# The experts' loads on SyncE: a program without a loop, its row numbers and words read one step ahead

## The reference, cut to what matters

```python
logits = x @ router_w + router_b                  # 8 experts
top_w, sel = jax.lax.top_k(logits, 2)
top_w = jax.nn.softmax(top_w, axis=-1)
...
gu = x @ Wgu + bgu                                # 128 -> 512
gate, up = jnp.split(gu, 2, axis=-1)
act = (up + 1.0) * quick_gelu(gate)
out = act @ Wd + bd                               # 256 -> 128
return (acc + out * w_e[:, None], None)           # only the two chosen experts have a weight
```

## Time and profile before

| | us |
|---|---|
| median of 3 runs | 1164.15 |
| the runs | 1164.15, 1156.54, 1166.43 |
| the profiled execution: its own time | 1155.15 |
| the profiled execution: span from the first to the last instruction | 1153.3 |
| PE busy over the span | 977.3 (85%) |
| DVE busy over the span | 837.6 (73%) |
| ACT busy over the span | 669.9 (58%) |

### The profile page before, as it was taken

The page is one execution under the profiler, slowest core; times in us unless marked ns, Lnnn a source line. Parts: engine busy times, 40 slices in busy tenths (PEclk is TensorE's granted clock), DMA queues, the critical chain, the costliest instruction groups (busy, mean ns, idle before and its releaser), DMA issues. The chain is left out here.

```text
span 1153.3 us, 41735 instructions
## 1 busy us (share of the span) xinstructions
PE 977.3 (85%) x14086; PEld 825.0 (72%) x14086; DVE 837.6 (73%) x2058; ACT 669.9 (58%) x1348; POOL 551.9 (48%) x588
## 2 busy tenths in 40 slices
PE   4799999899996788878888785179999999999995
PEld 3478877777775346666666664079898989889995
DVE  4687777677775246778787786358888888888885
ACT  1276666575661345666766663066676666666663
POOL 0327464647475712556556565414444444444444
PEclk9899999999999677899999997589999999999998
DMA  8011000001100200111121121556666666666661
GB/s 324 20 39 39 30 31 27 29 26 36 45 3 7 105 18 26 50 59 58 60 65 54 60 66 55 100 201 229 232 229 236 225 218 223 227 232 230 229 220 66
DMA packets 87673, 127.68 MB, mean 111 GB/s; under 512 B 12436, under 2 KB 53555, under 8 KB 87533
## 3 DMA queue, kind: packets, MB, share of 16 engines
q1 hardware_dynamic: 75116, 107.08, 26.8%
q0 software_dynamic: 9120, 17.15, 4.8%
q10 hardware_dynamic: 3298, 1.37, 0.8%
HBM read 31.61 MB, written 20.91 MB: 46 GB/s over the span
## 5 line engine op out<-in xcount | busy, mean ns | idle before, releaser
L1360 POOL DMA_INDIRECT out<-e_y,e_xg x156 | 155.6, 998 | 66.1 <-issue 66.1
L1413 PE MATMUL e_ps<-e_xt,weights 128*128 128x128 f16 x624 | 137.7, 221 | 25.6 <-DMA e_fed<-weights 16.5
L254 POOL TENSOR_SCALAR vm<-v,early 128x512 f32<-128x512 f32 x96 | 148.7, 1566 | 0.0
L820 POOL DMA_INDIRECT rows<-m_rows,m_place x128 | 126.9, 992 | 44.2 <-issue 44.2
L1415 PE MATMUL e_ps<-e_xt,weights 128*128 128x128 f16 x624 | 137.7, 221 | 0.0
L1414 PE MATMUL e_ps<-e_xt,weights 128*128 128x128 f16 x624 | 137.2, 220 | 0.0
L1413 PE MATMUL e_ps<-e_xt,e_fed 128*128 128x128 f16 x624 | 137.1, 220 | 0.0
L1414 PE MATMUL e_ps<-e_xt,e_fed 128*128 128x128 f16 x624 | 137.1, 220 | 0.0
L1415 PE MATMUL e_ps<-e_xt,e_fed 128*128 128x128 f16 x624 | 137.1, 220 | 0.0
L1494 DVE SCALAR_TENSOR_TENSOR e_hid<-e_ps,e_act 128x512 f32<-128x512 f32 x156 | 107.0, 686 | 27.9 <-ACT e_act L1479 16.1
L1500 DVE SCALAR_TENSOR_TENSOR e_hid_hl<-e_hid,e_hid_hl 128x512 f16<-128x512 f32 x156 | 108.1, 693 | 16.9 <-ACT e_hid_hl L1473 16.1
(11 more groups left out here) (262 smaller groups left out, 3098.0 us busy)
## 6 DMA issues: line engine op xcount, KB each, us to landing
e_fed<-weights SPq DMA_DIRECT2D x156, 416.0 KB
e_xg<-rows SPq DMA_DIRECT2D x156, 66.5 KB
resid<-in_x SPq DMA_DIRECT2D x8, 1024.0 KB, 14.2
xb<-in_x SPq DMA_DIRECT2D x32, 256.0 KB, 2.6
m_rows<-resid SPq DMA_DIRECT2D x32, 256.0 KB, 2.7
out<-e_y,e_xg POOLq DMA_INDIRECT x156, 3.3
m_w_f<-in_L_ffn_gate_up_proj SPq DMA_DIRECT2D x1, 2048.0 KB, 8.3
rows<-m_rows,m_place POOLq DMA_INDIRECT x128
```

Source lines behind the costliest of these rows:

```text
L254: ins = g.tensor_scalar(vm[:, u, :, n, :], full, pair_of[:, n:n + 1], None, ALU.mult)
L820: g.indirect_dma_start(rows_dram, bass.IndirectOffsetOnAxis(ap=place[:, slot, j:j + 1], axis=0), rows[:, slot, j, :], None).then_inc(s.row ...
L1360: nc.gpsimd.indirect_dma_start(out_rows, bass.IndirectOffsetOnAxis(ap=who, axis=0), y[:, slot, i, :], None, bounds_check=B * TOK - 1, oob_ ...
L1413: t.matmul(o, hi, x2[0], start=True, stop=False)
```

## The change

SP's loop becomes a program written out over all 80 steps of n. The limits of the `value_load`s are dropped, so nothing is checked behind them. The two row numbers of block n + 1 are read behind the two token DMAs of block n (the first two ahead of everything), and the word of the next 8 steps is read behind the last copy that needs the present one. The DMAs, their sizes, their order and the waits for semaphores are the same, with constant counts.

```diff
-            at = lambda n: slice(n, n + 1) if isinstance(n, int) else bass.ds(n, 1)
-            def load(n, slot, rounds):
-                need(sp, r_out[slot], 32 * rounds)
-                for half in range(2):
-                    row = sp.value_load(ffn["first_i"][0:1, half, at(n)], min_val=0, max_val=G * REGION)
-                    sp.dma_start(xg[:, slot, half], rows_dram[bass.ds(row, UNIT)]).then_inc(x_in[slot], 16)
...
-            def second_weights(k, ring, word, digit):
-                e = (word // 8 ** (digit + 1 - 2 * (digit % 2))) % 8
-                need(sp, s.y_psum, k - TURN + 1)
-                sp.dma_start(fed[:, ring:ring + 1], ffn["weights"][:, bass.ds(e, 1)]).then_inc(fed_in[ring], 16)
...
-            eight(0, 0, SLOTS, SLOTS)
-            with sp.Fori(1, BLOCKS // SLOTS) as m:
-                eight(m, 0, SLOTS, SLOTS)
-            for m in range(BLOCKS // SLOTS, -(-(BLOCKS + LEAD) // SLOTS)):
-                eight(m, 0, min(SLOTS, BLOCKS + LEAD - SLOTS * m), BLOCKS - SLOTS * m)
+            def rows_of(n):
+                return [sp.value_load(ffn["first_i"][0:1, half, n:n + 1]) for half in range(2)]
+            def second_words(turn):
+                return sp.value_load(ffn["word_i"][0:1, 1, turn:turn + 1])
+
+            coming, word = rows_of(0), second_words(0)
+            for n in range(BLOCKS + LEAD):
+                if n < BLOCKS:
+                    slot, here = n % SLOTS, coming
+                    need(sp, r_out[slot], 32 * (n // SLOTS))
+                    for half in range(2):
+                        row = here[half]
+                        sp.dma_start(xg[:, slot, half], rows_dram[bass.ds(row, UNIT)]).then_inc(x_in[slot], 16)
+                    if n + 1 < BLOCKS:
+                        coming = rows_of(n + 1)
+                for u in range(2 if n >= LEAD else 0):
+                    k = 2 * (n - LEAD) + u
+                    turn = (k + 2) // TURN
+                    digit = k - TURN * turn + BEHIND
+                    e = (word // 8 ** (digit + 1 - 2 * (digit % 2))) % 8
+                    need(sp, s.y_psum, k - TURN + 1)
+                    sp.dma_start(fed[:, k % TURN:k % TURN + 1], ffn["weights"][:, bass.ds(e, 1)]).then_inc(fed_in[k % TURN], 16)
+                    if (k + 3) // TURN > turn:
+                        word = second_words(turn + 1)
```

More of the change, by code:

```diff
@@ L1306, in _ @@
         def _(sp):
-            at = lambda n: slice(n, n + 1) if isinstance(n, int) else bass.ds(n, 1)
-            def load(n, slot, rounds):
-                need(sp, r_out[slot], 32 * rounds)
-                for half in range(2):
-                    row = sp.value_load(ffn["first_i"][0:1, half, at(n)], min_val=0, max_val=G * REGION)
-                    sp.dma_start(xg[:, slot, half], rows_dram[bass.ds(row, UNIT)]).then_inc(x_in[slot], 16)
-            def second_words(turn):
-                return sp.value_load(ffn["word_i"][0:1, 1, at(turn)], min_val=0, max_val=64 ** 5 - 1)
```

## The result

| | before | after |
|---|---|---|
| median of 4 runs, us | 1161.52 | 1141.35 |
| lowest and highest run | 1156.54, 1166.43 | 1139.03, 1143.06 |
| the profiled execution: its own time | 1155.15 | 1141.94 |
| its span | 1153.3 | 1140.0 |
| SP's first load of the experts (start) | 746.38 | 748.46 |

A forecast was written before the change was run, and what follows sets the result against it. SP's issuing and PE were taken to share the bound in the experts' stage, SP slightly above PE's floor. PE's cycles 12.0 plus start 0.9 made 12.9 us, put under the median 1164.15: 1151.2 us, range 1141 to 1161.

The forecast's parts named there:

- SP as the bound, PE's floor behind it: Experts' stage: SP, hardly waiting, keeps the pace at 4.94 us a block, a little above PE's floor of 4.74.
- SP's new work: SP in the experts' stage: 0.91 us of 4.94 a block goes, leaving 4.03, or 3.5 with short loads.
- their place: SP's row loads: behind token DMAs instead of a weight copy they might take 0.28 us each, not 0.552.
- The new wait on the scatter: SP's token DMAs: waits for block n-8's scatter, a microsecond or so a block; costs nothing, 5 us left over.
- the rival on the slower side: The new scatter wait binds if a scatter takes about 10 us to land; 1190 us at 12; chance 0.04.
- Hidden anyway: Copies late from landing time, or unchecked numbers cost as much as checks: gain 0 to 3 us, about 1163; chance 0.16.
- the look-ups: PE's 18 cycles between look-ups fall from 19.73 towards 18.95 us: 14.0 if all are short, 12.0 taken.
- I let a third of the look-ups stay long: PE's look-ups: a third still meet weight copies in flight, taking 2.0 off the 14.0 us gain.
- the first rival: PE's look-ups stay as long as they are: gain 9.0 us, time 1155; chance 0.27.
- the start: Start of the experts' stage: first weight copy issued 1.2 us earlier; gain 0.9, from 0.6 to 1.2 given PE's clock.
- the way from the profiled execution to the median: The 12.9 us gain, read from one execution of 1155.15, is put under the median 1164.15, giving 1151.2 us.
- the sum's 1142.3: Whole kernel: the time the profiled execution of 1155.15 us would take after the 12.9 us gain.

The follow-up runs named there:

- p_unchecked: The kernel before with only the limits of SP's two loads dropped, loop and places of the loads as before: 1142.97 us, ratio 0.9863.
- p_written: The kernel before with only SP's loop written out, limits and places of the loads as before: 1144.03 us, ratio 0.9869.
- p_written_early: The changed kernel with the limits of the loads put back, so written out, loads in their new place, checked: 1146.84 us, ratio 0.9894.
- pad2: The changed kernel with two more register loads and their arithmetic a block on SP, ahead of the weight copies: 1145.38 us, ratio 0.9893.
- pad6: The changed kernel with six more register loads and their arithmetic a block on SP, ahead of the weight copies: 1242.48 us, one run.
- a_again: The changed kernel, unchanged, run and profiled once more: 1140.00 us.
- b_third: The kernel before, unchanged, run for a third profile: 1160.45 us.
- loads_behind: The changed kernel with the next block's row loads moved from ahead of the two weight copies to behind them: 1142.30 us, ratio 0.9849.

## Why the prediction was right, and where it missed

**SP as the bound, PE's floor behind it: right, shown.** SP's absence of waits and the common pace of SP and PE were read correctly. `p_unchecked`, `p_written` and `p_written_early` come down to one cycle by three ways, and `pad2` and `pad6` show that SP costs next to nothing up to about 4.75 us a block and sets the pace beyond it. The floor itself, 18.95 from three cycles, was measured as 18.97. That an engine without waits runs at its own speed held for the kernel before, but not as a rule: in `p_written_early` and `pad2` SP hardly waits either, and PE's floor paces them.

**SP's new work: right.** 3.5 to 4.0 us were expected, 3.71 measured, and `pad6` bears that out, 6.04 where 3.71 and the padding make 6.05; the arithmetic on numbers without limits showed no cost. The loads behind the token DMAs are short, as expected, though the reason given for it, their place, is only part of it.

**The new wait on the scatter: right that it costs nothing.** It is there, 36.8 us in 34 waits or 0.47 us a block, about half of the "microsecond or so" that was forecast; SP's other wait, 43.3 us, is for the ring of weights. Behind it no copy comes late but the first, so the rival on the slower side has no sign in the profile. It wasn't tried with slower scatters.

**Hidden anyway: refuted.** The Trainium skill, "DMA: Bandwidth & Descriptors", section "Issuing engines are not separate DMA queues", calls the time that a sequencer needs to initiate a DMA usually small beside the DMA. For one copy this trace agrees, 0.50 us to issue and 2.78 to land. What fails is the conclusion that such time is hidden: four issues a block and the register work around them were the bound, and from `pad2` to `pad6` each further load cost 0.30 us a block.

**Term of the sum: the look-ups, mis-sized by 1.6 us.** "I let a third of the look-ups stay long" took 2.0 off the cycles. They gave 18 x (19.73 - 18.97) = 13.6, not 12.0: 2 of 19 are long. With that the first rival falls, too.

**Term of the sum: the start, 1.8 us instead of 0.9 in this pair.** From SP's first load to the second look-up it was 770.01 - 746.38 = 23.6 us and is 770.34 - 748.46 = 21.9. Of this, 1.3 is PE's earlier first step. Most of the rest, 0.5, is the clock's and not the change's: PE's first steps run at the lower level, 1.2 GHz, and how many of them do so differs between executions. Here the lower level lasted until 760.8, so the window has its rise at the end:

```profile
757.70:760.97 3.27, 3.27 (x30) 3.20 (x31) 0.43 (x1) 0.67 (x2) 0.00 (x0) 0.52 0.61 218
```

In `a_again`, the same kernel with nearly the same wait for the first copy, 4.0 us, it was still at 0.50 over the first 4.8 us:

```profile
755.04:759.80 4.76, 4.75 (x43) 4.69 (x44) 1.64 (x3) 1.87 (x4) 0.00 (x0) 0.50 0.73 249
```

In all five profiles of the two kernels the clock rises between 759.6 and 760.9 us of the span, while PE's first step comes anywhere between 755.0 and 757.9. So an earlier first step finds the lower clock for longer, as the prediction reckoned when it took 0.9 out of 0.6 to 1.2. In `a_again` the second look-up comes 22.5 us behind SP's first load, so against the first profile of before the start gains 1.1 there. What sets the moment of the rise stays open.

**The step that failed: the way from the profiled execution to the median.** The prediction says that "the stage that changes gives no reason why slower runs should gain less" and puts the 12.9 under the median. The stage does give a reason why they gain more. In the two slower executions PE waited 19.4 and 20.5 us for copies instead of 16.5, the cycles were longer, 19.97 and 20.05, and all of them come down to the same floor. For those the cycles alone give 18 x 1.00 to 18 x 1.08, 18.0 to 19.4 us, beside 13.6 for the one that was read. Over three profiles of before and two of after, the stage goes from 410.3 to 391.9 on average, 18.4 us; the medians differ by 20.2. The remaining 1.8 us lie within what the unchanged stages differ by: in the runs of this study the experts begin between 742.2 and 750.9 us. By the floor the forecast is a value of its own and not a difference to the median: the sum's 1142.3 for the profiled execution would have stood for the others too, and 1141.35 was measured. That 1141.35 still lies within the range is luck as far as this step goes: the lower end came from the lowest run less the full gain, not from the floor. Part of the way is seen in `b_third`, whose SP loop ran slower, 282.8 us in 56 blocks or 5.05 each, against 4.95 over the same 56 blocks of the execution that the prediction read:

```profile
L1342 SPq COMPARE_BRANCH  x8: 40/45/53, 816.3 to 1099.1; - x8
```

Of these 0.10 us, 0.06 lie in the issues of the copies and 0.03 in the row loads. Why those took longer in one execution than in the next stays open.

## What to carry to other kernels

A sequencer that never waits can be a bound, even if the page counts it as idle: compare its time per block with the floor of the busiest engine, read from cycles without a late transfer. The missing waits alone don't prove it, since issues can take up the slack. As soon as it is under that floor, further savings on it bring next to nothing, and the next gain lies in the same kind of register work on the engine that holds the floor. When a change removes what makes executions differ, all of them end at the floor: forecast the floor, not a difference to the median.

## What the runs showed of the hardware

- A register load from SBUF took 0.26 to 0.30 us at the least, on SP and on PE. Behind the issue of a 416 KB copy from SBUF to SBUF it was often longer, 732 ns in the median of `loads_behind` and 764 in `pad6`, but 273 at such a place in the changed kernel. In one window with a DMA share of 0.92, most of it a scatter's, a look-up of PE took 302 ns; in one with 1.01, nearly all of it from SP's queue, 585.
- A check of two register instructions behind each of PE's look-ups cost 0.31 us a cycle: without it PE's listed waits for "issue" fell from 8.4 to 1.8 us.
- The issue of a token DMA took 341 ns in the median, but up to 1.8 us. Two of them cost 0.79 us a block in the kernel before and 1.17 to 1.22 where SP ran ahead almost without listed waits.
- PE's first steps behind a wait of 4 us ran at a granted clock of 0.50 for about 3 us in one execution and almost 5 in another of the same kernel. In the kernel before, a wait of 2.0 us for one late copy was followed by a clock of 0.56 over 3.9 us.
